# Context products of the first token group: two runs of 128 columns in place of one of 256

## The chip, the cores and the metric

The kernel runs on one core of one Trainium2 chip. The metric is the device time of one execution in microseconds. Times are given as the median of several executions; the profile is of one further execution, which has a time of its own.

## The reference, cut to what matters

One decoder layer in float32 over 16 sequences of 128 tokens (2048 tokens, model width 256): causal self-attention with 16 heads of 64 on the tokens taken as 4 sequences of 512, then cross-attention to a context of the same shape, then a mixture of 8 experts (two per token) with a shared expert; each part is followed by a residual sum and a layer norm. The change is in the cross-attention, whose mask leaves one key to each query, as there are as many keys as queries:

```python
mask = j_idx % n_q == i_idx
sim = jnp.where(mask[None, None, :, :], sim, max_neg)
attn = jax.nn.softmax(sim, axis=-1)
out = jnp.einsum('bhij,bhjd->bhid', attn, v)
return out @ Wout + bout
...
x = _layernorm(x + xattn(x, ctx_1024, Wq, Wkv, Wout, bout))
```

With one key left, the softmax is 1 at that key, so what is added to token i is `ctx[i] @ Wv @ Wout + bout`. The kernel computes the product of the weights once (`wvo`, 256x256) and then, for each tile of 128 tokens, `ctx @ wvo + bout`. These are the context products.

## The kernel before, in words

The tokens are worked in four groups of 512 (`G = 4`, `g` from 0 to 3), each of four tiles of 128 tokens. Attention goes through a fixed program of slots (`all_slots`): one slot is one pair of heads of one group, in which TensorE (PE) issues the values product of an earlier pair (line 874), the scores (line 824), the transposes of the probabilities (line 835) and projections (lines 310 to 312); VectorE (DVE) and ScalarE (ACT) do the mask, the exponential and the copies out of PSUM. The order on each engine is written out by hand; engines meet at semaphores only.

Float32 products are made of three products of rounded halves (`three`, lines 310 to 312): each operand is split into a high and a low part of type float32r, and high by high, high by low and low by high are added in PSUM. One call of `pe.matmul` gives one LDWEIGHTS (shown as engine PEld: the stationary operand, 128 columns here) and one MATMUL (the moving operand, as many columns as the output has) when the operands are float32r; plain float32 operands give two of each.

Between slots, other work is put at fixed places: `behind` (after a slot), `soon` and `mid` (inside one). `behind[after(g, 0)]` holds `cross(g, 0)` and `behind[after(g, 1)]` holds `cross(g, 1)` (lines 1059 and 1060), with `after(g, r) = 8 g + 9 + r`. `cross(g, half)` (line 878) makes the context products of two tiles: for each tile j, a first matmul that puts the bias row into the output (`sel` by `rows[:, BOUT]`, line 893) and, for each half k of the 256 inputs, the three matmuls of lines 310 to 312, whose stationary operand is a 128-token tile of the context (`xt_hi`, `xt_lo`) and whose moving operand is 256 columns of `wvo_hi` or `wvo_lo`. That is 7 matmuls of 256 columns for a tile, 14 for a call, 28 for a group. All go to PSUM bank 7; the call ends with an increment of `cross_done`. On DVE `add_cross(g, half)` (lines 1608 to 1622) waits for it and adds the product to the residual; it is issued inside the slot `after(g, 1)` or `after(g, 2)`, and its increment of `cross_added` is what PE's `cross(g, 1)` waits for before it writes the bank again. DVE's rounds of small steps between the maxima of line 1478 (`root`, lines 1578 to 1592) stand ahead of `add_cross` in its queue.

Other lines that are spoken of below: `route` (line 919), gate logits from 8 moving columns with a new 128-column float32 tile as stationary operand each time; `cross_weights` (line 775), plain float32 products of 256 columns; line 945, counts in bfloat16 with 8 moving columns; DVE's `list_counts` (lines 1694 to 1732) in the last slots; POOL's split of the normalised tokens (line 587).

Of the kernel before, what the change touches and what calls it, by code (L numbers as in the profile page):

```python
# [15 lines left out]
P = 128  # L16
SEQS, S, D = 16, 128, 256
HEADS, DH = 16, 64
TOK = SEQS * S
KT = D // P  # L20
GROUP = 512
G = TOK // GROUP
GT = GROUP // P
# [40 lines left out]
BOUT = NX  # L64
# [4 lines left out]
def slices(i, n):  # L69
    return slice(i * n, (i + 1) * n)  # L70


def decoder_program(nc, x, x_t, ctx_t_in, w_quads, w_cross, w_experts, w_gate, col_bias, row_bias, down_bias,
                    out):
    st = ExitStack()
    with st:
        def sb(name, shape, dt=F32):
            return st.enter_context(nc.sbuf_tensor(name, shape, dt))
# [5 lines left out]
        xt_hi = sb("xt_hi", [P, KT, TOK], F32R)  # L84
        xt_lo = sb("xt_lo", [P, KT, TOK], F32R)
# [10 lines left out]
        rows = sb("rows", [P, NX + 1, D], F32R)  # L96
        sel = sb("sel", [P, 2, P], F32R)

        ex_raw = sb("ex_raw", [P, 2, KT * D])
        wvo_hi = sb("wvo_hi", [P, KT, D], F32R)  # L100
        wvo_lo = sb("wvo_lo", [P, KT, D], F32R)
# [37 lines left out]
        start = sb("start", [P, 2 * NE + 1])  # L139
# [28 lines left out]
        n = TOK // P  # L168
# [24 lines left out]
        n = LATER * 2 * NE  # L193
# [18 lines left out]
        cross_bank = [(bank[7], bank[7])] * (G - 1) + [(bank[5], bank[6])]  # L212
# [95 lines left out]
        def three(pe, o, a_hi, a_lo, b_hi, b_lo, first, last):  # L308

            pe.matmul(o, a_hi, b_hi, start=first, stop=False)  # L310
            pe.matmul(o, a_hi, b_lo, start=False, stop=False)  # L311
            return pe.matmul(o, a_lo, b_hi, start=False, stop=last)  # L312
# [404 lines left out]
        def _(pe):  # L717
# [160 lines left out]
            def cross(g, half):  # L878
                if half == 0:
                    pe.wait_ge(ctx_split, g + 1)  # L880
                    if g == 0:
                        pe.wait_ge(wvo_lo_ready, 1)
                        pe.wait_ge(rows_ready, NX + 1)
                        pe.wait_ge(sel_ready, 1)
                    elif g < G - 1:
                        pe.wait_ge(place_ready, g)
                elif g < G - 1:
                    pe.wait_ge(cross_added, 2 * g + 1)
                if g == G - 1:
                    pe.wait_ge(o_added, 2 * UNITS - 5 + half)  # L890
                for j in range(2):
                    o = cross_bank[g][half][:, slices(j, D)]
                    pe.matmul(o, sel[:, 0, :], rows[:, BOUT, :], start=True, stop=False)
                    for k in range(KT):
                        tok = slices(g * GT + 2 * half + j, P)
                        mm = three(pe, o, xt_hi[:, k, tok], xt_lo[:, k, tok], wvo_hi[:, k, :], wvo_lo[:, k, :],
                                   False, k == KT - 1)
                mm.then_inc(cross_done, 1)

            def x2_turn(g, k):  # L900
# [157 lines left out]
            for g in range(G - 1):  # L1058
                behind.setdefault(after(g, 0), []).append(lambda g=g: cross(g, 0))
                behind.setdefault(after(g, 1), []).append(lambda g=g: cross(g, 1))  # L1060
            soon, mid = {}, {}
            for g in range(G - 1):
                soon.setdefault(after(g, 4), []).append(lambda g=g: x2_turn(g, 0))
                mid.setdefault(after(g, 4), []).append(lambda g=g: x2_turn(g, 1))
                behind.setdefault(after(g, 4), []).append(lambda g=g: route(g))
                (soon if g == G - 2 else behind).setdefault(after(g, 5) + (g == G - 2), []).append(lambda g=g: rank(g))
            behind.setdefault(SLOTS - 2, []).append(lambda: cross(G - 1, 0))
            mid.setdefault(SLOTS - 1, []).append(lambda: cross(G - 1, 1))
            behind[SLOTS] = [lambda: shared_up(0, range(1)), lambda: values(Slot(SLOTS + 1)),
# [45 lines left out]
            def scaled(g, j, c, diagonal):  # L1115
                return pe.matmul(rows_of(g, j), diagonal, yg[g][c][:, j, :], start=False, stop=(c == 1 and j % 2 == 1))
# [12 lines left out]
            for j in range(0, GT, 2):  # L1129
                as_they_are(ON_PE, j)  # L1130
                for t in (j, j + 1):
                    for c in range(2):
                        mm = scaled(ON_PE, t, c, scale_by[t][c])
# [5 lines left out]
            for c in range(2):  # L1139
                pe.wait_ge(in_y[G - 1][c], 16)  # L1140
                for t in range(2):
                    mm = scaled(G - 1, GT // 2 + t, c, scale_last[t][c])
# [940 lines left out]
```

## Time and profile before

| | us |
|---|---|
| median of 3 runs | 459.45 (458.13 to 461.33) |
| the profiled execution | 459.26 |
| its span, first to last instruction | 457.5 |

The mean granted clock of TensorE in the profiled execution was 0.986 of full speed. In the views, a start is in microseconds from the start of the span; a duration of a MATMUL contains its way through the array, so that matmuls that follow each other overlap in the record, and the cost of one in a stream is read from the distance between starts (or ends) of neighbours. A timeline row of an engine that had sat idle ends with the idle time and its releaser in brackets; a row without brackets shows no wait.

### The profile page before, as it was taken

How to read it: one execution, taken by the hardware profiler on the slowest of the kernel's cores; microseconds unless marked ns; L12 is line 12 of the kernel's file. 1: busy time of each engine (PE TensorE's matmuls, PEld its weight loads, DVE VectorE, ACT ScalarE, POOL GpSimd, SP SyncE). 2: the span in 40 equal slices, each digit the busy share in tenths (PEclk: the TensorE clock that was granted, in tenths of full speed). 3: DMA queues.
4: the chain of work that ended last, by engine and by line, in shares of the span. 5: the costliest groups of instructions: out<-in, count | busy, mean ns of one | idle time of the engine just before them, and what ended most of it. 6: DMA issues, size and time to landing. Idle time of an engine off the chain costs nothing.

```text
span 457.5 us, 11055 instructions
## 1 busy us (share of the span) xinstructions
PE 438.9 (96%) x3657; PEld 396.5 (87%) x3657; DVE 307.1 (67%) x1243; ACT 300.6 (66%) x927; POOL 211.2 (46%) x246
## 2 busy tenths in 40 slices
PE   8999999999999999999999999997989999999981
PEld 7889898988989889898998988996888999999961
DVE  3376676778786766688675869699686725333485
ACT  3688656676766766668676566856464686776535
POOL 1899598440205011210156564288503587566521
PEclk9999999999999999999999999999799999999997
DMA  5950121400300001020011314022202654343675
GB/s 156 322 183 0 63 93 46 142 0 1 122 20 0 2 13 36 25 71 0 1 48 48 93 59 126 1 71 81 83 1 79 176 165 148 117 129 121 207 256 203
DMA packets 26543, 40.16 MB, mean 88 GB/s; under 512 B 3199, under 2 KB 17683, under 8 KB 26483
## 3 DMA queue, kind: packets, MB, share of 16 engines
q1 hardware_dynamic: 21532, 27.86, 19.7%
q0 software_dynamic: 3408, 9.33, 5.7%
q10 hardware_dynamic: 1547, 2.27, 1.7%
q8 instruction: 31, 0.51, 0.5%
q14 instruction: 25, 0.20, 0.2%
HBM read 26.83 MB, written 12.61 MB: 86 GB/s over the span
## 4 chain that ended last, share of the span: by engine, by line
PE 83%; DVE 8%; DMA 3%; ACT 2%; issue 1%; SPq 1%; POOL 1%; ACTq 0%; POOLq 0%
PE bank L310 17%; PE bank L311 17%; PE bank L312 17%; PE bank L824 7%; PE bank L874 7%; PE bank L835 7%; DMA ex_raw<-y_dram 3%; PE bank L1041 2%; PE bank L1017 2%; PE bank L775 2%; PE bank L919 1%; PE bank L752 1%; PE bank L1027 1%; DVE probs L1489 1%; PE bank L909 1%
## 5 line engine op out<-in xcount | busy, mean ns | idle before, releaser
L1204 ACT ACTIVATE probs<-probs,negmax 128x128 f32<-128x128 f32 x256 | 99.7, 393 | 24.5 <-DVE negmax L1478 24.5
L1478 DVE CUSTOM_DVE_ANT_0 probs<-bank,mask 128x128 f32<-128x128 f32 x256 | 62.3, 285 | 45.4 <-PE bank L824 45.4
L310 PE MATMUL bank<-w_hi,ot_hi 128*128 (+1 forms) x284 | 80.9, 285 | 0.0
L311 PE MATMUL bank<-w_lo,ot_hi 128*128 (+1 forms) x284 | 80.6, 284 | 0.0
L312 PE MATMUL bank<-w_hi,ot_lo 128*128 (+1 forms) x284 | 80.4, 283 | 0.0
L310 PE MATMUL bank<-xt_hi,w_hi 128*128 128x512 f32 (+1 forms) x148 | 60.0, 405 | 0.0
L1489 DVE TENSOR_TENSOR probs<-probs,rsum 128x512 f32<-128x512 f32 x64 | 58.3, 912 | 2.2
L311 PE MATMUL bank<-xt_lo,w_hi 128*128 128x512 f32 (+1 forms) x148 | 58.0, 392 | 0.0
L312 PE MATMUL bank<-xt_hi,w_lo 128*128 128x512 f32 (+1 forms) x148 | 58.0, 392 | 0.0
L611 POOL DMA_INDIRECT xg_dram<-xacc,place x32 | 33.5, 1047 | 52.2 <-PE bank L835 29.6
L1216 ACT ACTIVATE ot_hi<-bank,cols 128x512 fp32r<-128x512 f32 x32 | 22.0, 686 | 51.8 <-PE bank L874 51.8
L310 PEld LDWEIGHTS bank<-w_hi,ot_hi 128*128 128x128 f32 x284 | 54.5, 192 | 0.1
L312 PEld LDWEIGHTS bank<-w_hi,ot_lo 128*128 128x128 f32 x284 | 54.5, 192 | 0.0
L311 PEld LDWEIGHTS bank<-w_lo,ot_hi 128*128 128x128 f32 x284 | 54.3, 191 | 0.1
L1167 ACT ACTIVATE qkv<-bank,cols 128x512 f32<-128x512 f32 x64 | 43.7, 684 | 10.5 <-PE bank L312 10.2
L1204 ACT ACTIVATION_READ_ACCUMULATOR probs<-probs,negmax 128x1 f32 x256 | 48.6, 190 | 0.0
L1851 DVE TENSOR_TENSOR ot_lo<-bank,ot_hi 128x256 fp32r<-128x256 f32 x39 | 16.5, 424 | 45.0 <-ACT ot_hi L1315 45.0
L310 PE MATMUL bank<-w_hi,xt_hi 128*128 128x256 f32 x160 | 46.7, 292 | 0.0
L634 POOL DMA_INDIRECT y_dram<-qkv,w_raw x39 | 40.1, 1029 | 13.3 <-ACT qkv L1335 7.2
L311 PE MATMUL bank<-w_lo,xt_hi 128*128 128x256 f32 x160 | 44.7, 279 | 0.0
L312 PE MATMUL bank<-w_hi,xt_lo 128*128 128x256 f32 x160 | 44.7, 279 | 0.0
L874 PE MATMUL bank<-probs_t,qkv 128*64 128x128 f32 x512 | 35.9, 283 | 3.1 <-DVE ot_lo L1504 2.8
(247 smaller groups left out, 1062.1 us busy)
## 6 DMA issues: line engine op xcount, KB each, us to landing
qkv<-xg_dram SPq DMA_DIRECT2D x39, 128.5 KB, 2.1
ex_raw<-in_w_experts SPq DMA_DIRECT2D x18, 256.0 KB, 2.7
w_raw<-in_w_quads SPq DMA_DIRECT2D x10, 256.0 KB, 4.6
xacc<-in_x SPq DMA_DIRECT2D x4, 512.0 KB, 4.5
ex_raw<-in_w_cross SPq DMA_DIRECT2D x4, 512.0 KB, 3.9
w_raw<-in_ctx_t_in ACTq DMA_DIRECT2D x4, 512.0 KB, 3.8
w_raw<-in_w_quads SPq DMA_DIRECT2D x3, 512.0 KB, 6.3
xacc<-in_x_t SPq DMA_DIRECT2D x3, 512.0 KB, 6.4
```

The source lines that it names most:

```text
L310: pe.matmul(o, a_hi, b_hi, start=first, stop=False)
L311: pe.matmul(o, a_hi, b_lo, start=False, stop=False)
L312: return pe.matmul(o, a_lo, b_hi, start=False, stop=last)
L611: pool.indirect_dma_start(xg_dram, bass.IndirectOffsetOnAxis(ap=place[:, g, i, j:j + 1], axis=0), xacc[:, g * GT + j, :], None).then_inc(s ...
L634: pool.indirect_dma_start(y_dram, bass.IndirectOffsetOnAxis(ap=target[:, i:i + 1], axis=0), yt[:, i % YR, :], None).then_inc(y_sent[i % YR ...
L824: mm = pe.matmul(sc_bank[h][:, slices(j, P)], qt[s.ub][rows_h, s.pp, slices(j, P)], kt[s.ub][rows_h, s.pp, slices(j, P)], start=True, stop ...
L835: mm = pe.transpose(tr_bank[h][:, slices(j, P)], probs[:, 1 - s.par, h, slices(j, P)], ident[:, :])
L874: mm = pe.matmul(pv_bank[slices(h, DH), slices(j, P)], vb[:, j, c:c + DH], probs_t[:, h, slices(j, P)], start=True, stop=True)
L1167: nc.scalar.activation(dst, pj_bank[f % 2][:, :], ACT.Identity, bias=cols[:, b:b + 1]).then_inc(qk_ready, 1)
L1204: nc.scalar.activation(tile, tile, ACT.Exp, scale=-1.0, bias=negmax[:, s.par, h, j:j + 1], accum_out=sums[:, s.par, h, j:j + 1]).then_inc( ...
L1478: nc.vector.tensor_tensor_reduce(probs[:, s.par, h, slices(j, P)], sc_bank[h][:, slices(j, P)], mask[:, :], -SCALE, 3.0e38, ALU.add, ALU.m ...
L1489: nc.vector.tensor_tensor(tile, tile, rsum[:, h, :].unsqueeze(2).to_broadcast([P, GT, P]), ALU.mult).then_inc(probs_ready, 1)
```

## The change

In `cross`, for group 0 alone, the 256 output columns of a tile are made in two runs of 128 columns (`n = P`), each with its own bias matmul and its own six products; for the other groups `n` is 256 and the loop over `h` has one turn. The semaphores stay where they were: the waits ahead of the first matmul of a call, the increment on the last.

```diff
                 for j in range(2):
-                    o = cross_bank[g][half][:, slices(j, D)]
-                    pe.matmul(o, sel[:, 0, :], rows[:, BOUT, :], start=True, stop=False)
-                    for k in range(KT):
-                        tok = slices(g * GT + 2 * half + j, P)
-                        mm = three(pe, o, xt_hi[:, k, tok], xt_lo[:, k, tok], wvo_hi[:, k, :], wvo_lo[:, k, :],
-                                   False, k == KT - 1)
+                    n = D if g > 0 else P
+                    for h in range(D // n):
+                        o = cross_bank[g][half][:, j * D + h * n:j * D + (h + 1) * n]
+                        pe.matmul(o, sel[:, 0, :], rows[:, BOUT, slices(h, n)], start=True, stop=False)
+                        for k in range(KT):
+                            tok = slices(g * GT + 2 * half + j, P)
+                            mm = three(pe, o, xt_hi[:, k, tok], xt_lo[:, k, tok], wvo_hi[:, k, slices(h, n)],
+                                       wvo_lo[:, k, slices(h, n)], False, k == KT - 1)
                 mm.then_inc(cross_done, 1)
```

On PE, before the change, `cross(0, 0)` begins behind the output projections (`ot_hi`, `ot_lo`) of the slot; the first tile of two and the start of the second read (the last figure is stationary rows by moving columns):

```order
L312 MATMUL bank<-w_hi,ot_lo 128x256
L893 MATMUL bank<-rows,sel 128x256
L310 MATMUL bank<-wvo_hi,xt_hi 128x256
L311 MATMUL bank<-wvo_lo,xt_hi 128x256
L312 MATMUL bank<-wvo_hi,xt_lo 128x256
L310 MATMUL bank<-wvo_hi,xt_hi 128x256
L311 MATMUL bank<-wvo_lo,xt_hi 128x256
L312 MATMUL bank<-wvo_hi,xt_lo 128x256
L893 MATMUL bank<-rows,sel 128x256
```

After the change the same place holds, for the first half of the first tile's columns and the start of the second half (line 893 is now 895):

```order
L312 MATMUL bank<-w_hi,ot_lo 128x256
L895 MATMUL bank<-rows,sel 128x128
L310 MATMUL bank<-wvo_hi,xt_hi 128x128
L311 MATMUL bank<-wvo_lo,xt_hi 128x128
L312 MATMUL bank<-wvo_hi,xt_lo 128x128
L310 MATMUL bank<-wvo_hi,xt_hi 128x128
L311 MATMUL bank<-wvo_lo,xt_hi 128x128
L312 MATMUL bank<-wvo_hi,xt_lo 128x128
L895 MATMUL bank<-rows,sel 128x128
```

Each run of seven is now there twice, with half the columns: a call has 28 matmuls and 28 weight loads in place of 14, and group 0 has 56 in place of 28. Nothing else moves on PE, and DVE, ACT, POOL and SP issue what they issued.

## Rows read from the trace of the kernel before

**Rows 1.** The page's head: span, and busy time of each engine.
```profile
span 457.5 us, 11055 instructions
## 1 busy us (share of the span) xinstructions
PE 438.9 (96%) x3657; PEld 396.5 (87%) x3657; DVE 307.1 (67%) x1243; ACT 300.6 (66%) x927; POOL 211.2 (46%) x246
```
**Rows 2.** The page's chain that ended last, shares of the span by engine.
```profile
PE 83%; DVE 8%; DMA 3%; ACT 2%; issue 1%; SPq 1%; POOL 1%; ACTq 0%; POOLq 0%
```
**Rows 3.** Waits of PE between 105 and 316 us: total, times, longest.
```profile
PE bank L874 <- DVE probs_t L1523: 0.3, 1, 0.3
```
**Rows 4.** Timeline of PE from 104.9 us, cross(0, 0): start, duration, line, operands, count.
```profile
105.17 0.28 PE L893 MATMUL bank<-rows,sel 128*128 128x256 f32 x1
105.29 0.28 PE L310 MATMUL bank<-wvo_hi,xt_hi 128*128 128x256 f32 x1
...
106.71 0.28 PE L312 MATMUL bank<-wvo_hi,xt_lo 128*128 128x256 f32 x1
```
**Rows 5.** Timeline of PE from 111.8 us, cross(0, 1) and what follows.
```profile
115.57 0.28 PE L893 MATMUL bank<-rows,sel 128*128 128x256 f32 x1
...
117.10 0.28 PE L312 MATMUL bank<-wvo_hi,xt_lo 128*128 128x256 f32 x1
117.31 1.09 PE L874 MATMUL bank<-probs_t,qkv 128*64 128x128 f32 x16
```
**Rows 6.** Timeline of DVE from 104 us, around add_cross(0, 0).
```profile
109.25 0.29 DVE L1478 CUSTOM_DVE_ANT_0 probs<-bank,mask 128x128 f32<-128x128 f32 x1 [0.76 <-PE bank L824]
...
114.05 0.88 DVE L1619 SCALAR_TENSOR_TENSOR xacc<-xacc,rstd,bank 128x256 f32<-128x256 f32 x2
```
**Rows 7.** Weight loads by shape: busy, mean ns of one, idle before.
```profile
L874 PEld LDWEIGHTS bank<-probs_t,qkv 128*64 128x64 f32 x512 | 28.1, 139 | 9.6 <-issue 7.1 <-DVE probs_t L1523 0.4
...
L919 PEld LDWEIGHTS bank<-gate,w_raw 128*128 128x128 f32 x64 | 7.5, 192 | 0.0
...
L310 PEld LDWEIGHTS bank<-wvo_hi,xt_hi 128*128 128x128 f32 x32 | 6.0, 188 | 0.1
...
L945 PEld LDWEIGHTS bank<-chosen,ones_b 128*128 128x128 bf16 x28 | 0.8, 96 | 0.0
```
**Rows 8.** Timeline of PE, route of the third group.
```profile
297.38 1.85 PE L919 MATMUL bank<-gate,w_raw 128*128 128x8 f32 x16
```
**Rows 9.** PE by shape from 297.3 us: busy, mean ns of one.
```profile
L919 PE MATMUL bank<-gate,w_raw 128*128 128x8 f32 x16 | 1.8, 251 | 0.0
```
**Rows 10.** Timeline of PE from 68 us: cross_weights, then the values product.
```profile
67.65 0.81 PE L775 MATMUL bank<-ex_raw 128*128 128x256 f32 x3
68.39 1.09 PE L874 MATMUL bank<-probs_t,qkv 128*64 128x128 f32 x16
```
**Rows 11.** Line 775 on PE: duration ns min/median/max.
```profile
L775 PE MATMUL bank<-ex_raw x32: 377/379/381, 45.5 to 78.5; 128*128 128x256 f32 x32
```
**Rows 12.** Timeline of DVE from 313.6 us.
```profile
313.85 3.23 DVE L1697 TENSOR_SCALAR count<-count 128x8 f32<-128x8 f32 x1
...
317.52 0.21 DVE L1697 TENSOR_SCALAR count<-count 128x8 f32<-128x8 f32 x1
```
**Rows 13.** Timeline of POOL from 310 us.
```profile
314.51 2.54 POOL L587 TENSOR_TENSOR xt_lo<-w_raw,xt_hi 128x512 fp32r<-128x512 f32 x2
```
**Rows 14.** Timeline of PE from 318.9 us.
```profile
318.95 1.98 PE L874 MATMUL bank<-probs_t,qkv 128*64 128x128 f32 x16 [2.85 <-DVE ot_lo L1504]
```
**Rows 15.** Stretches: length, busy by engine, granted clock (1.00 is full), DMA share, GB/s.
```profile
104.50:108.00 3.50, 3.50 (x39) 3.19 (x38) 3.44 (x9) 0.65 (x3) 0.00 (x0) 1.00 0.00 0
...
296.40:299.90 3.50, 3.50 (x40) 3.48 (x40) 2.66 (x9) 0.97 (x6) 3.42 (x3) 1.00 0.00 0
...
318.95:325.00 6.05, 6.05 (x29) 5.17 (x30) 3.04 (x13) 2.44 (x5) 4.73 (x5) 0.50 0.26 91
```

## The prediction, made before the changed kernel had run

> **What bounds the kernel now.** I read the page's head first: PE is busy 438.9 of the span's 457.5 us, DVE 307.1 [rows 1]. Busy alone proves nothing, so next comes the chain that ended last: 83% of it runs on PE, 8% on DVE [rows 2]. The reader is to see that the engine the change touches is the one the end is counted on. The question is then whether it is so at the place of the change, and for that I take PE's waits from 105 us (where the first context product stands) to 316 us: one wait, of 0.3 us [rows 3]. In these 211 us PE stops for nobody, so what is added to its queue at 105 us can be taken back by no later wait before 316 us.
>
> The place itself is in two timelines. In cross(0, 0) the first matmul starts at 105.17 and the fourteenth at 106.71: 13 steps in 1.54 us, 0.118 us for one [rows 4]. In cross(0, 1) it is 115.57 to 117.10, 1.53 us, the same 0.118; the values product follows at 117.31 with no idle time in brackets [rows 5]. Group 0's 28 context matmuls so hold PE for 28 x 0.118 = 3.30 us.
>
> **The change, part by part.** Removed: 28 matmuls of 256 columns, 3.30 us. Added: 56 matmuls of 128 columns, each with its own weight load, 28 more of each than before. The columns streamed in all are the same; everything hangs on what one matmul of 128 columns costs in a stream of float32r ones. The trace has none, so I bound it.
>
> *From below.* The cheapest spacing with 128 columns is that of the values product, 16 matmuls in 1.09 us: less the 0.28 that one matmul's passage takes [rows 4], 0.81 over 15 steps is 0.054 us [rows 10]. At that price 56 cost 3.0 us, a gain of 0.3 us. But those matmuls load 64 columns of weights and not 128.
>
> *The weight load.* One LDWEIGHTS of a context tile takes 188 ns, the route's float32 one 192, the values product's with half the columns 139, a bfloat16 one 96 [rows 7]. Halving the columns takes 49 ns off, so 128 columns stand for about 98 ns of a load (an estimate: 2 x 49), and the load is as long for a matmul of 128 columns as for one of 256. The nearest row that shows what happens when the load is longer than the stream is the route: a fresh 128-column 4-byte tile for each matmul, and only 8 moving columns. Its 16 matmuls take 1.85 us [rows 8]; less one of 0.25 us [rows 9], 1.60 over 15 steps is 0.107 us (0.105 to 0.112 by the rounding and by which matmul is taken off, as the last need not be a mean one). With hardly anything to stream, the loads alone keep matmuls 0.107 us apart, 9% less than the 0.118 of 256 columns. So halving the columns can't halve the step. I take 0.112 us, between the route's 0.107 and the 0.118 of today, nearer to neither, since 128 columns have some streaming that 8 have not: 56 x 0.112 = 6.27 us, +2.97 us. With 0.107 it is +2.7 us, with 0.118 +3.3 us.
>
> *From above.* The dearest spacing of 4-byte matmuls is that of plain float32 at full clock: three of line 775 in 0.81 us [rows 10], less one of 0.379 [rows 11], is 0.216 us for a step. At that price 56 cost 12.1 us, +8.8 us. Loads that hide nothing, 188 ns each one after another [rows 7], give 10.5 us, +7.2 us.
>
> What lies beside it: nothing takes the added time away. DVE's add_cross(0, 0) runs at 114.05, after the steps that the scores at 109.25 let go [rows 6]; those scores stand behind cross(0, 0) on PE and come later by the same 1.5 us, and so does cross(0, 1), which was 0.64 us behind the end of that addition or more (114.93 to 115.57) [rows 5, 6]. The wait on it stays covered. The slots behind move as a whole, with the engines that feed PE given 1.5 us more at each of the two places, which they don't need since PE doesn't wait for them. No DMA, queue or buffer is touched: both halves go to the bank that the tile had, and the semaphores come with the same matmuls.
>
> The granted clock was 1.00 at cross(0, 0) [rows 15] and 1.00 through the route, the stretch with the fewest streamed columns; the fall to 0.50 came only after PE had sat idle for 2.85 us [rows 14, 15]. Two calls of 3.1 us, without a gap in them, I cost at no loss of clock.
>
> The sum: the profiled execution's 459.26 us (span 457.5 and 1.8 around it) + 3.0 = 462.2 us. The median of the runs before is 459.45, 0.2 above that execution and inside their spread, so no correction. It is +0.65%, and about 1% is what a measurement of this kernel can tell from no change.
>
> The Trainium skill has a rule on either side of this. "TensorE: Matmul & The Clock Gate", section "LDWEIGHTS (loading the stationary operand)", gives a load's time as its columns over 1.2 GHz, 107 ns for 128: the route's 0.107 agrees. By it the sum would be 56 x 0.107, +2.7 us.
>
> **The rivals.**
>
> *The stream sets the step, no change.* If the loads hide behind one another, 128 columns cost half of 256: 56 x 0.059 = 3.30 us, 459.3 us. For it: the values product at 0.054 us [rows 10]. Against it: that has half the weights, and the route, with nearly no stream, doesn't get under 0.105 [rows 8, 9]. The same page of the Trainium skill, section "Back-to-back issue gap", has about 81 ns for a stream of load and matmul pairs at 128 columns, which would make the change cost 56 x 0.081 - 3.30 = 1.2 us, an estimate; no row here with 4-byte weights of 128 columns comes as close as that.
>
> *Short float32r runs lose the single pass, slower.* If a run below 256 columns goes at the rate of plain float32, a step is 0.216 us [rows 10, 11] and the end 459.3 + 8.8 = 468.0 us. For it: every float32r matmul of this kernel has 256 columns or more, so its rate below that is unseen. Against it: nothing in the trace speaks of such a threshold; the two instructions that a plain float32 matmul becomes are a property of its operands' type.
>
> *The load is exposed in part.* With half the stream to hide under, more of the 188 ns shows [rows 7]; all of it gives 459.3 + 7.2 = 466.4 us. Against it: the route's loads are as long and its step is 0.107.
>
> *The late collision goes, faster.* One DVE instruction of 128x8, line 1697, takes 3.23 us at 313.85 and its twin 0.21 [rows 12]; it ends at 317.08, and POOL's pair on line 587, which began 0.66 us behind it, at 317.05 [rows 13]. PE waits 2.85 us behind it and then works 6.05 us at half clock [rows 14, 15], which costs another 3.0. If the later group 0 shifts the two against each other by more than that 0.66 us, so that the small instruction is through before POOL's pair begins, 5.9 us come back: 462.2 - 5.9 = 456.3 us. Against it: both hang on the same PE program, which moves as a whole.
>
> **How the numbers follow.** Forecast (a step of 0.105 to 0.125 us, nothing else moved) 0.70; stream sets the step 0.06; single pass lost 0.14; load exposed 0.06; collision gone 0.04. The predicted time is 462.2. The range goes down to the stream case, 459.0 with the spread of the runs, and up to the exposed loads, 466.8; the lost pass and the collision, 0.18 together, are left out. Slower by over 1% (above 464.0): lost pass 0.14, exposed load 0.06, and 0.03 of the forecast for noise or a fall of the clock: 0.23. Faster by over 1%: half of the collision's 0.04, as its 456.3 falls short of 454.9 by itself: 0.02. Within 1%: 0.75.
>
> **What would show it.** In the changed kernel's timeline, 28 matmuls from the first bias row of cross(0, 0) to its end should be 0.107 to 0.118 us apart and the call last 3.1 us in place of 1.65, twice; weight loads of 188 ns should follow each other without a gap. PE should still have no wait over 0.3 us between there and the end of the slots, and everything from 117 us on should start 3 us later, the wait before line 874 near 319 us included. A step near 0.059 or above 0.18 proves the forecast wrong at its one uncertain term. Steps as forecast with another total would put the error in the claim that nothing later gives or takes.

## The result, and the profile after

The changed kernel took 462.12 us (median of 13 runs, 460.81 to 464.34) against 459.24 for the kernel before in the same comparison (13 runs, 457.80 to 461.81): a ratio of 1.0062, 95% interval 1.0047 to 1.0077. It is slower by 2.9 us, less than 1%. The forecast was 462.2. The ratios here and below leave out three executions in the comparisons of experiments 9 and 10 (486 to 540 us), whose granted clock was far lower than in the others.

The page's head and chain of the profiled execution (462.12 us, span 460.4), which answer to [rows 1, 2]:

```profile
span 460.4 us, 11111 instructions
PE 441.1 (96%) x3685; PEld 398.4 (87%) x3685; DVE 312.1 (68%) x1243; ACT 300.6 (65%) x927; POOL 210.6 (46%) x246
PE 81%; DVE 12%; ACT 3%; DMA 2%; issue 1%; POOL 0%; ACTq 0%; SPq 0%; POOLq 0%; DVEq 0%
```

PE has 28 matmuls and 28 weight loads more; DVE, ACT and POOL have the same counts as before. The two calls in the timeline of PE, which answer to [rows 4, 5] (start, duration, line, operands):

```profile
106.91 0.22 PE L895 MATMUL bank<-rows,sel 128*128 128x128 f32 x1
106.97 0.28 PE L310 MATMUL bank<-wvo_hi,xt_hi 128*128 128x128 f32 x1
107.08 0.28 PE L311 MATMUL bank<-wvo_lo,xt_hi 128*128 128x128 f32 x1
107.20 0.28 PE L312 MATMUL bank<-wvo_hi,xt_lo 128*128 128x128 f32 x1
...
109.88 0.28 PE L312 MATMUL bank<-wvo_hi,xt_lo 128*128 128x128 f32 x1
110.08 1.09 PE L874 MATMUL bank<-probs_t,qkv 128*64 128x128 f32 x16
...
118.72 0.22 PE L895 MATMUL bank<-rows,sel 128*128 128x128 f32 x1
...
121.69 0.27 PE L312 MATMUL bank<-wvo_hi,xt_lo 128*128 128x128 f32 x1
121.89 1.09 PE L874 MATMUL bank<-probs_t,qkv 128*64 128x128 f32 x16
```

From the second matmul at 106.97 to the last at 109.88 are 26 steps in 2.91 us: 0.112 us for a matmul of 128 columns, where one of 256 took 0.118. A call lasts 3.17 us up to the values product (106.91 to 110.08, 118.72 to 121.89), where it lasted 1.75 and 1.74: 2.85 us more for the two, as against 2.88 us between the medians. No row of either call has idle time in brackets. The weight loads leave no gap, and the clock is full: in the stretch of the first call (length; PE, PEld, DVE, ACT, POOL busy; granted clock, DMA share, GB/s) PEld is busy 3.10 of 3.10 us.

```profile
106.90:110.00 3.10, 3.10 (x30) 3.10 (x28) 3.06 (x9) 0.00 (x0) 0.00 (x0) 1.00 0.02 5
```

This execution also differs from that of before at other places, which must not be read into the change. cross(0, 0) begins at 106.91 and not at 105.17, so 1.74 us had been lost before the changed instructions. That start differs from profile to profile, whatever the kernel: in the twelve profiles of this study it lies between 105.17 and 106.97, and the latest is that of experiment 5, whose context products are those of before. The values product behind the late wait begins at 324.56 and not at 318.95 [rows 14], 5.6 us later: the 1.74, the 2.85 and 1.0 more around 310 us. The end is 2.9 us later, so 2.7 us came back behind the wait. Of these, 1.25 us had come back by the transposes of line 909 (339.64 us before, 344.00 here), where the stretch at half clock was shorter: the granted clock was 0.50 over 318.95 to 325.00 before and 0.62 over 324.56 to 329.00 here. Why the rest came back is not shown. As single executions differ in these pieces, the medians are compared, and experiments 6 and 10 make the comparison again with other late slots.

### The profile page after: what moved, and what is told of

Read it like the earlier page. It is cut to its first block, busy times and chain, and to the rows that moved or that the text cites. A ratio compares the mean times of both kernels' runs of the same rounds, so it can differ in the third digit from the quotient of the medians.

```text
span 460.4 us, 11111 instructions
## 1 busy us (share of the span) xinstructions
PE 441.1 (96%) x3685; PEld 398.4 (87%) x3685; DVE 312.1 (68%) x1243; ACT 300.6 (65%) x927; POOL 210.6 (46%) x246
## 4 chain that ended last, share of the span: by engine, by line
PE 81%; DVE 12%; ACT 3%; DMA 2%; issue 1%; POOL 0%; ACTq 0%; SPq 0%; POOLq 0%; DVEq 0%
PE bank L310 17%; PE bank L311 17%; PE bank L312 17%; PE bank L824 7%; PE bank L874 6%; PE bank L835 6%; PE bank L1043 2%; PE bank L1019 2%; PE bank L775 2%; PE bank L921 1%; DVE xacc L1909 1%; DVE probs L1491 1%; DMA xacc<-in_x_t 1%; PE bank L1029 1%; DVE stats L1919 1%
## 5 line engine op out<-in xcount | busy, mean ns | idle before, releaser
L1491 DVE TENSOR_TENSOR probs<-probs,rsum 128x512 f32<-128x512 f32 x64 | 62.2, 971 | 2.2
```

What stands on the lines that cost most here:

```text
L1491: nc.vector.tensor_tensor(tile, tile, rsum[:, h, :].unsqueeze(2).to_broadcast([P, GT, P]), ALU.mult).then_inc(probs_ready, 1)
```

## The experiments

Two theories stood against each other at first: that a matmul of 128 columns costs its weight load (0.112 us, whatever streams), with PE waiting for nobody, and that the cost is something of short runs as such or a shift of other work. The experiments keep the numbers of their runs.

**Experiment 1: all four groups.** The condition on g goes:

```diff
-                    n = D if g > 0 else P
+                    n = P
```

> All four groups' context products in runs of 128 columns. Theory (each matmul of 128 columns costs one weight load, 0.112 us a step, and PE waits for nobody before the last slots): groups 0 to 2 cost 2.8 us each, 8.5 us together, and group 3 something from 0 to 2.8 us, as PE has a wait of 2.85 us behind it; 467.7 to 470.6 us, ratio 1.018 to 1.025. Rival (group 0's cost of 2.9 us in the median is for the most part a shift of the start or of the late slots and not the products): under 465 us.

Measured: 466.11 us against 459.1 of before, ratio 1.0145 (1.0118 to 1.0172), below the forecast and above the rival's 465 us. The calls of groups 0 to 2 lasted 3.16 or 3.17 us each and those of group 3 3.25 and 3.16 (1.83 and 1.73 before), so the price of the products held. Three groups at 2.85 us would make 8.55 us and 7.0 were measured, so the last group's products cost nothing on balance and a gain came with them. It stood at the end of the slots, where PE's wait for the low half of the attention output, 2.85 us before [rows 14], is now

```profile
328.17 1.09 PE L874 MATMUL bank<-probs_t,qkv 128*64 128x128 f32 x16 [0.71 <-DVE ot_lo L1506]
```

and the granted clock (the figure that follows the five engines' busy times) doesn't fall:

```profile
300.00:340.00 40.00, 38.54 (x355) 35.15 (x354) 32.30 (x130) 25.74 (x74) 27.79 (x27) 1.00 0.20 63
```

**Experiment 2: the last group alone.** Condition `n = D if g < G - 1 else P`.

> Group 3 alone in runs of 128 columns, group 0 as before. Its two calls stand at 302 and 306.7 us of the trace of before, behind the point where the chain that ended last leaves PE for DVE (302 us), and PE waits 2.85 us on DVE some 10 us later. Theory (an addition costs what no later wait takes back): the steps are 0.112 us, PE gets 2.8 us more work, the wait ahead of the values product shrinks by about as much, and the time is within 1 us of before, 458.2 to 460.2; it may be less if the granted clock then doesn't fall. Rival (PE is the bound to the end): 462 us as with group 0.

Measured: 457.94 us against 459.1, ratio 0.9975 (0.9958 to 0.9991). The same 2.85 us of work on PE, put at 303 and 309 us, makes the kernel slightly faster, a little below the expected 458.2. The timelines of DVE, POOL and PE of this run, which answer to [rows 12 to 14]:

```profile
316.84 0.39 DVE L1699 TENSOR_SCALAR count<-count 128x8 f32<-128x8 f32 x1
317.26 1.22 DVE L1702 TENSOR_SCALAR need<-count 128x8 f32<-128x8 f32 x1
...
315.92 2.54 POOL L587 TENSOR_TENSOR xt_lo<-w_raw,xt_hi 128x512 fp32r<-128x512 f32 x2 [0.44 <-DVE probs L1491]
...
320.14 1.09 PE L874 MATMUL bank<-probs_t,qkv 128*64 128x128 f32 x16 [0.69 <-DVE ot_lo L1506]
```

DVE's small step, 3.23 us long before, loses 0.2 us here and its successor 1 us, and PE waits 0.69 us (and 0.74 for the next low half, at 323.57). PE's added work stands where it would have waited, and DVE, which PE holds back a little, meets POOL's pair later and for a shorter time. The half clock behind the wait, 6.05 us before [rows 15], is gone too:

```profile
300.00:335.00 35.00, 33.57 (x310) 30.14 (x311) 30.60 (x121) 22.60 (x59) 23.78 (x26) 1.00 0.25 77
```

Set against the whole of experiment 1: three groups at 2.85 us less 1.16 here (459.1 - 457.94) make 7.4 us, 1.016, inside its interval.

**Experiment 3: runs of 192 and 64 columns** for group 0, still 56 matmuls.

```diff
-                    n = D if g > 0 else P
-                    for h in range(D // n):
+                    cuts = (0, D) if g > 0 else (0, 192, D)
+                    for c in (slice(a, b) for a, b in zip(cuts, cuts[1:])):
```

> Group 0 in runs of 192 and 64 columns, the same 56 matmuls. Theory (the load sets the step, whatever streams): 0.112 us for both lengths, a call 3.1 us, all as in the change. Rival (a run under 256 columns streams at half the rate, 0.107 us for 128 by its stream): 0.160 us for 192 columns and 0.107 or less for 64, a call 3.7 us.

Measured (one run, 461.17 us), in the timeline of PE:

```profile
106.00 0.28 PE L310 MATMUL bank<-wvo_hi,xt_hi 128*128 128x192 f32 x1
...
106.57 0.27 PE L312 MATMUL bank<-wvo_hi,xt_lo 128*128 128x192 f32 x1
...
106.73 0.28 PE L310 MATMUL bank<-wvo_hi,xt_hi 128*128 128x64 f32 x1
...
107.28 0.28 PE L312 MATMUL bank<-wvo_hi,xt_lo 128*128 128x64 f32 x1
```

Five steps of 192 columns take 0.57 us and five of 64 columns 0.55: 0.114 and 0.110, where the rival had 0.160 for the long ones. A factor of three in columns changes the step by 0.004 us.

**Experiment 4: 96 columns of weights.** As the change, but the stationary operand has 96 of the 128 tokens, so the last 32 tokens of each tile of group 0 get no product.

```diff
-                        o = cross_bank[g][half][:, j * D + h * n:j * D + (h + 1) * n]
+                        o = cross_bank[g][half][0:m, j * D + h * n:j * D + (h + 1) * n]
...
+                            tok = slice(at, at + m)
```

> Group 0 as in the change, but with 96 of the 128 tokens as stationary columns (the last 32 tokens of each tile of group 0 get no product). Theory (the time of the weight load, which goes by its columns, sets the step): 0.084 us a step, three quarters of 0.112, a call 2.4 us. Rival A (a fixed price for the issue of a load and matmul pair): 0.112 us. Rival B (the 128 columns' stream sets the step): 0.112 us.

Measured (one run, 460.08 us), first the timeline of PE, then the weight loads by shape (busy, mean ns of one):

```profile
106.05 0.25 PE L310 MATMUL bank<-wvo_hi,xt_hi 128*96 128x128 f32 x1
...
108.26 0.25 PE L312 MATMUL bank<-wvo_hi,xt_lo 128*96 128x128 f32 x1
108.43 0.43 PE L874 MATMUL bank<-probs_t,qkv 128*64 128x128 f32 x3
```

```profile
L312 PEld LDWEIGHTS bank<-wvo_hi,xt_lo 128*128 128x128 f32 x24 | 4.5, 188 | 0.0
...
L312 PEld LDWEIGHTS bank<-wvo_hi,xt_lo 128*96 128x96 f32 x16 | 2.6, 165 | 0.0
```

26 steps in 2.21 us are 0.085 us for one, as the theory had it (0.084), with the same 128 columns streamed and the same pairs issued. Neither the stream nor a price for the issue sets the step: the load does. Experiment 8, with 96 columns of weights and 256 streamed, asks the same of the other side:

> Group 0 in runs of 256 columns as before, but with 96 of the 128 tokens as stationary columns (the last 32 tokens of each tile of group 0 get no product). Theory (at 256 columns the stream is the longer of the two): 0.118 us a step, a call 1.75 us, unchanged. Rival (the load sets the step at 256 columns too): 0.09 us, a call 1.3 us.

Measured (one run, 458.19 us), in the timeline of PE:

```profile
106.86 0.28 PE L312 MATMUL bank<-wvo_hi,xt_lo 128*96 128x256 f32 x1
106.98 0.28 PE L310 MATMUL bank<-wvo_hi,xt_hi 128*96 128x256 f32 x1
107.10 0.28 PE L311 MATMUL bank<-wvo_lo,xt_hi 128*96 128x256 f32 x1
107.22 0.28 PE L312 MATMUL bank<-wvo_hi,xt_lo 128*96 128x256 f32 x1
```

0.12 us a step, a call of 1.74 us (1.75 for the second): unchanged by shorter loads, so at 256 columns the stream is the longer of the two. The 256-column run of the kernel before sits just above the point where the two meet (0.118 against 0.112).

**Experiment 7: four runs of 64 columns** for group 0, `n = D if g > 0 else P // 2`, 112 matmuls.

> Group 0 in four runs of 64 columns, 112 matmuls in place of 28. Theory (one load a matmul, whatever streams): 0.112 us a step, a call 6.3 us in place of 1.75, 9.1 us in all, 468.2 us, ratio 1.020. Rival (the cost goes with the columns below some number): a step of 0.06 to 0.09 us or of more than 0.13.

Measured: 475.07 us against 459.76, ratio 1.0343 (1.0312 to 1.0373), far over the expected 1.020. The step was 0.112 us as the theory had it, and then it was not:

```profile
108.68 0.28 PE L310 MATMUL bank<-wvo_hi,xt_hi 128*128 128x64 f32 x1
108.79 0.28 PE L311 MATMUL bank<-wvo_lo,xt_hi 128*128 128x64 f32 x1
108.90 0.28 PE L312 MATMUL bank<-wvo_hi,xt_lo 128*128 128x64 f32 x1
109.01 0.38 PE L310 MATMUL bank<-wvo_hi,xt_hi 128*128 128x64 f32 x1
109.21 0.40 PE L311 MATMUL bank<-wvo_lo,xt_hi 128*128 128x64 f32 x1
109.42 0.40 PE L312 MATMUL bank<-wvo_hi,xt_lo 128*128 128x64 f32 x1
109.64 0.40 PE L895 MATMUL bank<-rows,sel 128*128 128x64 f32 x1
```

From 109.01 on a step takes 0.213 us. The stretches show the clock behind it:

```profile
105.50:109.00 3.50, 3.50 (x34) 3.50 (x33) 3.30 (x11) 0.00 (x0) 0.00 (x0) 1.00 0.02 5
109.00:114.00 5.00, 5.00 (x26) 5.00 (x25) 0.00 (x0) 0.00 (x0) 0.00 (x0) 0.50 0.00 0
114.20:119.20 5.00, 5.00 (x38) 4.41 (x38) 0.84 (x9) 1.19 (x4) 0.00 (x0) 0.50 0.00 0
```

The granted clock fell from 2.4 to 1.2 GHz in the middle of the call, with PE and PEld at work in every moment, and stayed there up to about 119.2 us, through the values product, the scores and most of the transposes of the slot behind it. The second call, which begins at 125.21, lost its clock in the same way near 129.5. The two calls so took 8.7 and 8.0 us, 13.2 more than before in place of the expected 9.1. The work behind them lost 3.8 us more, most of it at half clock (10.97 us between the calls in place of 8.65, and 1.5 us behind the second), and in this execution about 2 us came back behind the late wait.

**Experiments 5 and 9: the late wait, taken away in two ways.** One rival had priced a collision of DVE and POOL near 314 us at 5.9 us. In experiment 5 POOL's pair is let go later:

```diff
-            pool.wait_ge(probs_ready, 2 * SLOTS)
+            pool.wait_ge(count_taken, 1)
             x2_lo(2)
```

> The kernel before (runs of 256 columns everywhere), but POOL's pair on line 587 for group 2 is let go by DVE's last step of list_counts and no longer by its last probabilities. Theory (DVE's small step of 3.2 us lasts until POOL's pair ends; without that, PE's wait of 2.85 us and the 6 us at half clock behind it go): the step takes under 0.5 us, PE waits under 1 us ahead of the values product, the granted clock stays at 1.00 there, and the time is 453 to 455 us, ratio about 0.99. Rival (the small step is slow for a reason of its own): as before, 459.

Measured: 458.73 us against 459.76, ratio 0.9980 (0.9965 to 0.9995). The small step is short and the clock of the profiled execution holds (1.00 over 300 to 335 us), but the expected 453 to 455 us are not reached. The timelines of DVE, POOL and PE:

```profile
316.85 0.17 DVE L1697 TENSOR_SCALAR count<-count 128x8 f32<-128x8 f32 x1
...
318.85 0.90 DVE L1738 TENSOR_TENSOR w_raw<-upto,need 128x64 f32<-128x64 bf16 x1
...
320.04 1.04 DVE L1707 TENSOR_TENSOR w_raw<-tile_no,ends 128x136 f32<-128x136 f32 x1
...
318.37 2.56 POOL L587 TENSOR_TENSOR xt_lo<-w_raw,xt_hi 128x512 fp32r<-128x512 f32 x2 [0.88 <-DVE count L1732]
...
323.97 0.36 PE L310 MATMUL bank<-w_hi,ot_hi 128*128 128x256 f32 x1 [2.21 <-DVE ot_lo L1504]
```

The 3.2 us hung on POOL's pair: with the pair moved to 318.37 us the step takes 0.17. But the collision has moved and is not gone. The pair now runs beside DVE's list of tiles, two steps of which take 0.90 and 1.04 us where they took 0.21 and 0.30 before, and PE waits 2.21 us for the next low half, which stands behind that list in DVE's queue. Experiment 9 therefore changes DVE's order:

```diff
-                if s.p >= SLOTS:
-                    flush(parts)
                 o_lo_first = s.p >= SLOTS - 2
```

> The kernel before (runs of 256 columns everywhere), but in DVE's last two slots the low half of the attention output (line 1504), for which PE waits, is issued ahead of the steps that count and list the expert tiles. Theory (the late wait of 2.85 us and the half clock behind it are DVE's order, not the context products): no wait of PE over 1 us between 300 and 335 us, granted clock 1.00 there, 453 to 456 us, ratio 0.986 to 0.993. Rival (the end hangs on DVE's list in any order): 0.997 or more.

Measured: 456.84 us against 459.68, ratio 0.9943 (0.9923 to 0.9963). This is 2.8 us faster than before by the medians and 2.6 by the ratio, just outside the expected 453 to 456 us, and faster than both kernels of the study. PE's waits in 300 to 335 us are now at most 1.3 us, the clock is full:

```profile
320.90 0.35 PE L310 MATMUL bank<-w_hi,ot_hi 128*128 128x256 f32 x1 [0.23 <-DVE ot_lo L1504]
333.73 0.39 PE L310 MATMUL bank<-w_hi,xt_hi 128*128 128x256 f32 x1 [1.29 <-DVE xt_lo L1815]
...
300.00:335.00 35.00, 32.76 (x294) 28.69 (x294) 32.35 (x125) 22.73 (x60) 24.61 (x26) 1.00 0.24 77
```

The bound on waits (1 us) was missed by 0.3: DVE works without idle time from its second low half (320.01 us) to the end of the split that PE waits for (333.68 us).

**Experiments 6 and 10: the change on both of these.** This is the change of the study once more, on kernels whose late slots run otherwise.

> The changed kernel (group 0 in runs of 128 columns) with the same edit on POOL. Theory (group 0's cost doesn't hang on the late wait): 2.8 us over the kernel with that edit alone, and steps of 0.112 us. Rival (a part of the 2.9 us came from where the late collision fell): under 2 us or over 4 us.

> The changed kernel with the same edit on DVE. Theory (group 0's cost is its 56 loads at 0.112 us and is taken back nowhere): 2.8 us over the kernel with that edit alone. Rival (it was partly the late wait and the clock behind it): under 2 us or over 4 us.

Measured: experiment 6 took 461.14 us, 2.4 over the kernel with POOL's edit alone, ratios 1.0031 (1.0012 to 1.0050) and 0.9980, so 0.5% apart. Experiment 10 took 459.64 us, 2.80 over the kernel with DVE's edit alone (2.4 by the ratios), ratios 0.9996 (0.9979 to 1.0012) and 0.9943. The second pair is the cleaner: its calls last 3.17 us against 1.74, and the clock doesn't fall in the slots of either, as this stretch of experiment 10 shows beside that of experiment 9 above:

```profile
300.00:335.00 35.00, 33.80 (x306) 29.90 (x305) 31.76 (x122) 23.00 (x65) 25.36 (x26) 1.00 0.27 77
```

In the first pair the clock of experiment 6 was 0.95 over the same stretch, behind the same wait of 2.21 us after which it held in experiment 5. With the late wait there, moved or gone, the change costs 2.4 to 2.9 us.

## Why the prediction was right

Step by step, as it was made:

- *PE is the bound at the place, and nothing takes the time back.* Right, with one sign missed: PE was to have no wait over 0.3 us up to the end of the slots, and had one of 0.54 near 313.7. Between the calls and the late slots PE's waits were

```profile
PE bank L310 <- DVE ot_lo L1506: 0.5, 1, 0.5
PE bank L874 <- DVE probs_t L1525: 0.3, 1, 0.3
```

  (in 105 to 319 us, where [rows 3] had the second alone). The longer one need not be the change's: it is there in kernels with runs of 256 columns too (0.72 us in experiment 5, 0.42 in experiment 9). Behind the calls, group 1's first context matmul came 4.58 us later than before (186.05 against 181.47), the 1.74 that were lost ahead of them and 2.84 of the calls. Experiments 6 and 10 gave nearly the same cost with other ends. Experiment 2 shows that the claim is one of place: 200 us later the same products cost nothing.
- *A step of 0.112 us for 128 columns, since each matmul brings a load.* Right, and the route's row with 8 columns was the right neighbour [rows 8]. The last digit is luck: 0.112 was taken between 0.107 and 0.118 because 128 columns have some streaming, and the runs show no such part, as 64 columns took 0.112 too (experiment 7 at full clock). That the load is the cause was argued then and is shown now: three quarters of the weights' columns gave three quarters of the step, and other stream lengths below 256 changed it by 0.004 us at most. By the change of 0.027 us for 32 columns a load of 128 is worth 0.108 us; the estimate from the durations in the trace of before (98 ns) was a little low. The Trainium skill, "TensorE: Matmul & The Clock Gate", section "LDWEIGHTS (loading the stationary operand)", with 107 ns for 128 columns, agrees. The calls of the kernel before last 1.75 us and not the 1.65 that the prediction gave, as 0.2 us pass between the last matmul and the values product; the calls of 128 columns have the same 0.2, so it drops out.
- *The stream sets the step* would have shown 0.059 us, *the single pass is lost* 0.216, *the load is exposed* 0.188 (its end is 459.3 + 7.2 = 466.5, where the prediction has 466.4). All three are refuted by the 0.112, and so is the 0.081 us a step that the first had as its other price; the middle one had the largest chance of the three and nothing in the trace for it. The cheap row that spoke for the first, 0.054 us [rows 10], was no neighbour of the change: its operands are plain float32, two matmuls to a product, and the two heads of a tile write one half each of the output's partitions. What makes those matmuls come so close is not tested here.
- *The clock holds at 128 columns.* Right (1.00 through both calls), but the reason given was too narrow, and luck had a part. The prediction tied a fall to an idle PE: with 64 columns the clock fell without one, and after the same wait of 2.21 us it held in one profile and fell in another (experiments 5 and 6). The calls of 128 columns were over after 3.17 us, sooner than those of 64 columns lost their clock (3.5 and 4.3 us from their starts), so no run shows whether a longer call of 128 columns would have kept it.
- *The collision stays where it is.* Right for group 0: the small step again took 3.24 us and PE waited 2.84. The price set on its going, 5.9 us, was wrong. It counted the wait and the half clock as if nothing stood behind them. Experiment 5 took the collision off the small step and gained 1.0 us, because the list steps that it met then lost 1.4 us and the next wait of 2.21 us came in place of the old one. It took another order on DVE to gain 2.8 us by the medians.

So the sum was right in its one uncertain term. The two things it left out, the later start of the calls and the late shifts of the profiled execution, differ from one execution to the next and don't show in the medians.

## What to carry to other kernels

In these runs, at full clock, a float32r matmul in a stream cost the longer of its stream and its weight load. With 128 columns of weights they meet a little below 256 moving columns (0.118 and 0.112 us), so that a run of 256 split in two took nearly twice as long (3.17 us a call in place of 1.75). Price an addition at the place where it stands: the same 56 matmuls cost 2.9 us where PE never waited and nothing where it was about to wait. Before a wait is priced as a gain, look at what is queued behind it on the engine that is waited for.

## What the runs showed of the hardware that was not expected

The granted clock can fall while TensorE is busy without a gap: in streams of 64 columns under full weight loads it went from 2.4 to 1.2 GHz in the middle of both calls of experiment 7. Calls of 128 columns kept 2.4 GHz, but they were shorter. At 1.2 GHz the load-bound step was 0.213 us in place of 0.112, so the load slows with the clock as the stream does. For the stream, these matmuls of 512 columns of the kernel before, at half clock behind its late wait, are four steps of 0.428 us, where the same ones at 110.20 to 115.34 us, at full clock, are 0.234 apart:

```profile
321.44 0.63 PE L311 MATMUL bank<-xt_lo,w_hi 128*128 128x512 f32 x1
...
323.15 0.63 PE L312 MATMUL bank<-xt_hi,w_lo 128*128 128x512 f32 x1
```

DVE and POOL: a step on 128x8 numbers took 3.2 us and ended with POOL's pair, at 317.08 against 317.05 before [rows 12, 13] and here, in the changed kernel's timelines of DVE and POOL, at 322.70 against 322.67:

```profile
319.46 3.24 DVE L1699 TENSOR_SCALAR count<-count 128x8 f32<-128x8 f32 x1
...
320.12 2.55 POOL L587 TENSOR_TENSOR xt_lo<-w_raw,xt_hi 128x512 fp32r<-128x512 f32 x2
```

Moved apart in experiment 5, it took 0.17. The Trainium skill, "SBUF — State Buffer", section "SBUF: two separate sides", has the two engines share a pair of ports, which the one that starts first holds for a whole instruction while the other stands still. The trace agrees in that one engine stands still until the other is done. It differs in the order: the small step waits out both instructions of POOL's pair, which began 0.66 us behind its own recorded start. At that start POOL was issuing a DMA (313.52 to 314.48 us in the kernel before). Whether the issue has a part in it, and whether the ports are the cause at all, no run here shows.
